# Two feed-forward layers with conditional mixing: NF4 levels by eight parametric ReLUs, condition matrices picked on VectorE

## The reference, cut to what matters

```
x = x + ffn0(cond0(x));   x = x + ffn1(cond1(x))
cond:  W = weights[condition]          # 16 matrices of 64x64; condition: one code 0..15 for each of 32 batches
       y[b] = W[b]^T x[b]              # einsum('bct,bcd->bdt')
ffn0:  y @ (ternary(w) * column scale) + b       # w 1024x1024
ffn1:  w = NF4_LEVELS[q_weight] * group scale    # q_weight 1024x1024 int32, codes 0..15; 64 values to a group
       y @ w^T + bias + 4 * lora
```

## Time and profile before

| | |
|---|---|
| time, 3 runs | median 371.6 us (371.12 to 373.02) |
| the profiled execution | 371.03 us, of which the span of the trace is 369.2 us |
| PE busy | 354.6 us (96%) |
| DVE, ACT, POOL busy | 243.3, 169.6, 228.3 us |
| mean granted TensorE clock | 0.994 |

### The profile page before, as it was taken

The page is one execution under the profiler, slowest core; times in us unless marked ns, Lnnn a source line. Parts: engine busy times, 40 slices in busy tenths (PEclk is TensorE's granted clock), DMA queues, the critical chain, the costliest instruction groups (busy, mean ns, idle before and its releaser), DMA issues.

```text
span 369.2 us, 5527 instructions
## 1 busy us (share of the span) xinstructions
PE 354.6 (96%) x1832; PEld 299.9 (81%) x1832; DVE 243.3 (66%) x361; ACT 169.6 (46%) x302; POOL 228.3 (62%) x147
## 2 busy tenths in 40 slices
PE   7999987999999999998989999999999999999996
PEld 6788875878888888887868888888888888888885
DVE  4996457587997887974699999846155362544522
ACT  4775647678888778882021323504013040231300
POOL 0769999956886878667443302386468464685642
PEclk9999999899999999999999999999999999999999
DMA  7994400554246146333331133021405014150202
GB/s 212 309 306 142 148 22 29 193 211 146 96 167 199 45 156 216 117 114 114 127 119 57 61 120 114 18 101 62 174 36 180 22 70 166 57 175 4 114 30 85
DMA packets 27838, 44.63 MB, mean 121 GB/s; under 512 B 8834, under 2 KB 17026, under 8 KB 27810
## 3 DMA queue, kind: packets, MB, share of 16 engines
q1 hardware_dynamic: 26466, 43.95, 34.9%
q10 hardware_dynamic: 1344, 0.33, 0.4%
HBM read 27.49 MB, written 16.78 MB: 120 GB/s over the span
## 4 chain that ended last, share of the span: by engine, by line
PE 73%; DVE 10%; ACT 6%; issue 4%; POOL 4%; DMA 1%; SPq 1%; DVEq 0%; POOLq 0%; ACTq 0%
PE acc L1177 31%; PE acc L1139 20%; PE xT L1103 9%; PE acc L1119 7%; PE spare L1103 3%; DVE plain_sums L927 3%; ACT spare L721 2%; POOL x_first L557 2%; DVE side_p L908 2%; DVE hl L865 2%; ACT hh L673 1%; PE acc L1204 1%; DMA mix<-in_L_cond_weights 1%; PE acc L1103 1%; POOL side_p L584 1%
## 5 line engine op out<-in xcount | busy, mean ns | idle before, releaser
L551 POOL TENSOR_TENSOR X<-X,bias 128x1024 f32<-128x1024 f32 x28 | 69.1, 2468 | 34.1 <-PE xT L1103 26.6
L1139 PE MATMUL acc<-T,hh 128*128 128x512 f32 x192 | 75.9, 396 | 0.0
L1139 PE MATMUL acc<-T,hl 128*128 128x512 f32 x192 | 75.0, 391 | 0.0
L721 ACT ACTIVATE spare<-q_mid 128x512 f32<-128x512 int8 x96 | 55.5, 596 | 13.6 <-DVE side_p L908 6.6
L1177 PE MATMUL acc<-W,hh 128*128 128x512 f32 x192 | 61.1, 389 | 0.0
L1103 PEld LDWEIGHTS xT<-mix,X 128*128 128x128 f32 x352 | 43.7, 197 | 7.4 <-issue 6.4
L1103 PE MATMUL xT<-mix,X 128*128 128x128 f32 x352 | 44.6, 282 | 4.2 <-DVE hl L865 4.1
L1010 DVE TENSOR_TENSOR X<-X,acc 128x512 f32<-128x512 f32 x36 | 24.7, 687 | 32.9 <-PE acc L1177 18.6
L1177 PEld LDWEIGHTS acc<-W,hh 128*128 128x128 f32 x192 | 36.0, 188 | 7.5
L1139 PEld LDWEIGHTS acc<-T,hl 128*128 128x128 f32 x192 | 36.1, 188 | 7.4
L1139 PEld LDWEIGHTS acc<-T,hh 128*128 128x128 f32 x192 | 36.1, 188 | 7.0
(11 more groups left out here) (97 smaller groups left out, 662.5 us busy)
## 6 DMA issues: line engine op xcount, KB each, us to landing
out<-X SPq DMA_DIRECT2D x26, 512.0 KB, 3.1
X<-out SPq DMA_DIRECT2D x16, 512.0 KB, 3.4
X<-in_x SPq DMA_DIRECT2D x12, 512.0 KB, 3.4
q_raw<-in_L_ffn_q_weight SPq DMA_DIRECT2D x16, 256.0 KB, 2.9
w_in<-in_L_ffn_w SPq DMA_DIRECT2D x15, 256.0 KB, 5.2
x_first<-in_x SPq DMA_DIRECT2D x4, 512.0 KB, 5.2
out<-x_first SPq DMA_DIRECT2D x4, 512.0 KB, 5.8
out<-X SPq DMA_DIRECT2D x4, 256.0 KB, 2.0
```

The costliest lines, as they stand in the source:

```text
L551: pool.tensor_tensor(x_of(g), x_of(g), bias[:, :], ALU.add).then_inc(s_xb, 1)
L721: act.activation(dst, q_mid[:, parity, :], ACT.Copy, scale=slope, bias=offset).then_inc(s_line, 1)
L1139: mm = pe.matmul(acc[:, bank_of(q), :], a[:, k, :], b, start=(k == 0 and j == 0), stop=(k == KB - 1 and j == len(terms) - 1))
```

## The change

Two things are changed together.

Codes to levels: a piece is now 128 x 1024, eight pieces in all, and ACT runs a chain of eight parametric ReLUs over it, each with its own scale, offset and slope below zero; the last one gives the levels. DVE has no part in it any more and POOL only multiplies by the scales. `turn_w` writes both halves into `spare`, and `high_w` and `low_w` take 1024 columns at once. acc uses its four banks in turn for all tiles of layer 0.

Condition matrices: the whole table of a layer (16 x 64 x 64) is loaded into both halves of the partitions. `tok` is loaded into all partitions, DVE compares it with 0 to 15 (`choose`), and `pick` copies, for each of the 16 conditions, the table's matrix into `picked` where the mask says so: 32 predicated copies for a group of tiles (one of 64 columns for a tile in the first two groups of two tiles, of 128 columns in the groups of four). ACT then copies the group to the diagonal blocks of `mix`, which now has 8 places (`place`, two operations).

```
+    GROUPS = [(0, 2), (2, 4)] + [(g, g + 4) for g in range(4, 2 * NT, 4)]
+    NPICK = 2 * NCOND
...
+            def place(i):
+
+                a, b = GROUPS[i]
+                act.wait_ge(s_picked, NPICK * (i + 1))
+                if i == 0:
+                    act.wait_ge(s_fill, 1)
+                need(act, s_xT, NH * (b - NM))
+                for h in range(2):
+                    rows = slice(h * C, (h + 1) * C)
+                    act.activation(mix[rows, a % NM:a % NM + b - a, rows], picked[rows, 0:b - a, :],
+                                   ACT.Copy).then_inc(s_mix, 1)
...
+                    act.activation(lev, src, ACT.Prelu, scale=scale, bias=offset, alpha=below
+                                   ).then_inc(s_lev, 1)
...
             act.preload_act_table(ACT.Sign)
-            act.wait_ge(s_tok, 16)
-            act.wait_ge(s_fill, 1)
-            load_condition(act, 0, 1)
-            load_condition(act, 1, 1)
+            load_table(act, mix0, 1)
             load_weights(act, 2, 0)
             act.dma_start(b_raw[:, :, :], lora_b_v).then_inc(s_bin, 16)
+            place(0)
+            place(1)
             signs(0, 0)
...
-            act.wait_ge(s_ain, 64)
-            act.activation(loraA[:, :], a_raw, ACT.Copy).then_inc(s_ah, 1)
-            per = (2 * NL + 1) * ND
+            per = NS * ND
+            place(group_of(F))
             for g in range(SB):
                 if g == 1:
                     colscale(1)
+                    act.wait_ge(s_ain, 64)
+                    act.activation(loraA[:, :], a_raw, ACT.Copy).then_inc(s_ah, 1)
...
+            def pick(i, start=0, stop=NPICK):
...
+                for u in range(start, stop):
+                    c, part = divmod(u, 2)
+                    t = a % NT + n * part
+                    mine = chosen[:, c, t:t + n].unsqueeze(2).to_broadcast([P, n, C])
+                    if c > 0:
+                        dve.wait_ge(s_picked, NPICK * i + u - 1)
+                    dve.copy_predicated(picked[:, n * part:n * part + n, :], mine,
+                                        table[:, c, :].unsqueeze(1).to_broadcast([P, n, C])
+                                        ).then_inc(s_picked, 1)
...
+            choose()
+            pick(0)
+            pick(1)
             ternary(0, 0)
...
             leave_y(2)
-            per = 2 * NC * ND
+            pick(group_of(F))
...
-                    if g < NT:
-                        maxima(share(per, m), share(per, m + 1))
-                    else:
+                    for i, (a, b) in enumerate(GROUPS):
+                        if a >= 2 * F and a - 4 <= g <= a - 3:
+                            at = NPICK // 4 * (m - NH * (a - 4))
+                            pick(i, at, at + NPICK // 4)
...
                 if p + 1 < NP:
                     low_A(p + 1, A22, 1)
+                if (SB + 2 * p + 4, SB + 2 * p + 8) in GROUPS:
+                    pick(group_of(SB + 2 * p + 4))
```

More of the change, by code:

```diff
@@ L42, with nf4_stages_are_right @@
 NF4_ZERO = 7
-def line_through(a, level_a, b, level_b):
-    f = np.float32
[L49 to L82, removed]
+NF4_STAGES = [(0.300930947, -1.00947642, 1.30589235), (0.999999046, -3.25468516, 0.532812595),
+              (1.00000417, 0.568540156, 0.82866317), (1.00000179, 0.706044614, 1.09465003),
+              (0.999996901, -1.0337441, 0.641103864), (0.999999702, 0.375342011, 0.934238434),
+              (0.999999046, 0.679873884, 2.33418441), (1.0, -0.545852602, 1.14412689)]
+def nf4_stages_are_right():
+    f = np.float32
+    for q in range(len(NF4_LEVELS)):
+        y = f(q)
+        for scale, offset, below in NF4_STAGES:
+            y = f(float(y) * float(f(scale)) + float(f(offset)))
+            y = y if y > 0 else f(y * f(below))
+        assert abs(float(y) - float(f(NF4_LEVELS[q]))) <= float(np.spacing(abs(f(NF4_LEVELS[q])))), q
+        assert y == 0 or q != NF4_ZERO
 def build(nc, x, itok, mix0, w0, b0, mix1, q_weight, q_scale, b1, lora_a, lora_b, out):
@@ L121, in build @@
     NP = (2 * NT - SB) // 2
-    assert C * 2 == P and NH == 2 and ND == NT and G == 16 and R == 8
-    above, below = nf4_lines()
+    assert C * 2 == P and NH == 2 and G == 16 and R == 8
+    nf4_stages_are_right()
     x_v = x.rearrange("(t s) c f -> t (s c) f", s=2)
@@ L174, in ready_in, with begun_in @@
     def ready_in(d):
-        return next(m for m in range(NH * NT) if share(2 * NC * ND, m + 1) >= 2 * NC * (d + 1))
+        return next(m for m in range(NH * NT) if share(NS * ND, m + 1) >= NS * (d + 1))
+    def begun_in(d):
+        return next(m for m in range(NH * NT) if share(NS * ND, m + 1) > NS * d)
     def turned_in(d):
@@ L210, in build @@
         mix = sb("mix", [P, NM, P], F32)
+        table = sb("table", [P, NCOND, C], F32)
+        with ExitStack() as first_use:
+            number = sb("number", [P, NCOND], I32, first_use)
+        picked = sb("picked", [P, 4, C], F32)
+        with ExitStack() as first_use:
+            ones = sb("ones", [P, P], F32, first_use)
         loraA = sb("loraA", [P, T], F32R)
@@ L321, in build @@
         s_bin = sem("s_bin")
-        s_qin = [sem(f"s_qin{k}") for k in range(2)]
+        s_qin = sem("s_qin")
         s_zero = sem("s_zero")
@@ L511, in _ @@
                     load_x(g + 3)
+                if g == 10:
+                    sp.wait_ge(s_picked, NPICK * G0)
+                    load_table(sp, mix1, 0)
+                    load_table(sp, mix1, 1)
+                for d in range(2, ND):
+                    if begun_in(d - 1) // NH == g:
+                        load_q(d)
             sp.wait_ge(s_xb, NT)
@@ L840, in _ @@
                                        ).then_inc(s_loraB, 1)
+                if g >= F and (g + 2, g + 6) in GROUPS:
+                    place(group_of(g + 2))
                 for m in (NH * g, NH * g + 1):
@@ L849, in _ @@
                     if g < NT:
-                        lines(share(per, m), share(per, m + 1))
+                        stages(share(per, m), share(per, m + 1))
                     else:
```

214 lines of the change are left out of this document (86 added, 128 removed).

## The result

| | before | after |
|---|---|---|
| median of 4 runs | 371.36 us (370.8 to 373.02) | 409.57 us (407.74 to 412.17) |
| profiled execution, its span | 371.03, 369.2 us | 407.74, 405.9 us |
| PE busy | 354.6 us (96%) | 365.8 us (90%) |

The ratio is 1.103 (95% interval 1.095 to 1.110): 38.2 us slower where 19.9 were forecast, and outside the range of 374 to 402.

The account below looks back on a forecast made before the run. PE, busy 354.6 of 369.2 us, was taken to set the end. Start, tiles 4 to 7, low clock and first rounds gave 19.2, later stalls -3.7, boundaries +4.4: 19.9 on 371.0, so 391.0 us, range 374 to 402.

Parts of the forecast that it names:

- Start, +8.65: Kernel start: table landing at 6.0 and 64 copies at 0.14 us delay the first sign; PE's first(0,0,1) 8.65 us later.
- Tiles 4 to 7, +8.95: At turn_b: copies held beside POOL delay ACT's place and colscale(1), so PE waits 8.95 us more.
- Low clock behind it, +1.7: After the wait at turn_b: PE wakes at the low clock level, costing 1.7 us.
- mixed(5), -1.66; scaled weights, -1.6; mixed(6), +3.2: First loop rounds: mixed(5)'s wait goes, the scaled-weights stall shrinks by 1.6 us, mixed(6) waits 3.2 us for its low part.
- Loop copies 0 (0 to 4): Loop: DVE, having lost 96 maxima, absorbs the copies at about zero cost, 0 to 4 us.
- Later stalls, -3.7: Later in the kernel: the stalls of 0.7, 1.3 and 1.78 us go, 3.7 us gained.
- Pair boundaries, +4.4: Boundaries between pairs: copies for tiles 24 and 28 delay freeing a bank, 2.2 us each, 4.4 us.
- 1 (DVE keeps the port): Tiles 4 to 7: overlapping copies never release the port, so POOL waits 6.6 us; 382.3 us, chance 0.2.
- 2 (no clash): Copies beside POOL: the mask is read another way, so nothing is held; 374.9 us, chance 0.17.
- 3 (faster): Whole kernel: relief exceeds the start's price, with 64-column copies in 0.075 us; 364.8 us, chance 0.1.
- Rival 4: All groups: as forecast, but each copy takes the full 0.25 us; about 405 us, chance 0.08.

Follow-up runs that it names:

- e3: Changed kernel with 4 copies in place of 32 in each of the first two groups; 403.18 us.
- f4: Changed kernel with the products' banks moved on by one and 4 copies in place of 32 in every group; 367.04 us.
- e8: Changed kernel with POOL waiting for the 32 copies of tiles 4 to 7 ahead of its first add_bias; 407.83 us.
- e4: Changed kernel with 4 copies in place of 32 in the group of tiles 4 to 7; 400.59 us.
- h3: Changed kernel with the products' banks moved on by one and 32 small matmuls on PE ahead of the wait for the column scale; 400.46 us.
- i2: Changed kernel with the products' banks moved on by one and 4 copies in place of 32 in the groups of tiles 8 to 19; 395.03 us.
- f6: Changed kernel with the products' banks moved on by one and 4 copies in place of 32 for tiles 20 to 23; 398.54 us.
- i3: Changed kernel with the products' banks moved on by one and 4 copies in place of 32 in the groups of tiles 8 to 23; 392.26 us.
- f1: Changed kernel with condition matrices loaded by DMA as before, Relu for parametric ReLU, and the products' banks moved on by one; 363.45 us, ratio 0.979 to before.
- i1: Changed kernel with the banks of the seven products moved on by one, timed; 402.4 us, ratio 1.084 to before.
- f3: Changed kernel with the banks of the seven products moved on by one, a single run; 402.88 us.
- h2: Changed kernel with the products' banks moved on by one and one wide copy per condition in place of two; 410.44 us.

## Why the prediction was wrong

Two steps failed. The copies in the loop were put at zero and cost 4 to 6 us where DVE was already full, and the relief of 3.7 us didn't show behind them. The bank of the last result was no term of the sum at all; it cost 4.3 us at its place. Going by its own steps:

- *Start, +8.65.* Right in kind, +10.8 at tile 3. The copies cost what was taken (0.136 from start to start for 0.14). The landing of the table was taken at 6.0 from the first weights and came at 7.7, and the second group's wait for `place(0)` (0.8) was overlooked. e3 and f4 split it: some 7.4 us are the copies, 3.4 the table and the rest.
- *Tiles 4 to 7, +8.95.* Right, and the step that was least certain. +10.2 from tile 3 to tile 4 is the wait of 8.07 and the low clock behind it. e8 shows the mechanism, e4 the amount.
- *Low clock behind it, +1.7.* There, but worth nothing at tile 6 (h3): the chain that sets mixed(6) runs over ACT, POOL and DVE and not over PE. The forecast's +19.2 at tile 6 doesn't hang on it, though. Without the 1.7 PE reaches the first scaled piece at 76.8 and not at 78.5, waits 2.7 for it and not 1.0, and all that follows stands where it stood. That is what h3 shows, 2.3 us of waiting for 0.4. So the spell changed the terms of the sum and not the sum. The wait of 8 us was right to count, because that same chain stood behind the same copies.
- *mixed(5), -1.66; scaled weights, -1.6; mixed(6), +3.2.* Right: 84.0 forecast for mixed(6), 84.78 measured; +19.9 for +19.2. A part of that closeness is luck: the copies of tiles 4 to 7 began 2.0 us later than forecast (43.26 for 41.3) and took 0.8 less (14.37 for 15.2).
- *Loop copies 0 (0 to 4).* Wrong. For tiles 12 to 19 it holds (under 1 us at tile 17 in i2). For tiles 20 to 23 it doesn't: 4 to 6 us (f6, i3). The copies are dealt out by tile, the last ones fall into tiles 16 and 17, and there DVE begins the block sums at 93% busy. "DVE has lost its 96 maxima and absorbs that" is true for tiles 8 to 13 and false behind it, since no maxima stood there. The earlier trace rows had shown the stage; its busy share was not read.
- *Later stalls, -3.7.* The relief is real: f1 is 8.1 us below before, where the three terms of relief made 7.0. In the changed kernel it doesn't show after tile 17, because DVE's lag replaced the stall of 1.78 at tile 18.
- *Pair boundaries, +4.4.* Right in place and mechanism; the two waits are 2.13 each for 2.2. The copies took 298.95 - 292.93 = 6.02 us after POOL's end, for 6.0. With the low clock behind each they cost 6.5 us in the changed kernel (tiles 22 to 28) and in i1, 4.9 in f3 and 4.8 in h3.
- *Missing: the bank of the last result.* 4.3 us at tile 22, and 7 us of the time as measured (1.103 to 1.084). The change to `bank_of` was in the diff, and only its first-layer half was taken up.

From tile 6 to the end the sum is: 0.7 ahead of it, 9.6 between tiles 6 and 21 (+5.9 instead of -3.7), 4.3 at the bank, 2.1 more at the boundaries: 16.7, the whole distance between +36.6 and +19.9. The median of four runs stands 1.8 us above the profiled one; that makes the rest.

Of the rivals, 1 (DVE keeps the port), 2 (no clash) and 3 (faster) are out by the rows above: POOL's operations stay at 2.45 and 1.40, the copies take 14.37 us. Rival 3's 0.075 us a copy was 0.136. Rival 4 (405) came nearest, for the wrong reason: the copies do overlap. The rule cited in the prediction, of the Trainium skill ("VectorE: DVE Perf Modes", The DRAIN you can't avoid), would have made the start's copies 0.22 apart; they are 0.136 apart. But the prediction quoted half of it: the same section says that a next operation which isn't held starts earlier, and that is what these rows show. By the other ("SBUF — State Buffer", Who interferes with whom) an instruction with two SBUF inputs shares an exclusive lock with GpSimd, and the trace agrees for a predicated copy too, which the page doesn't name: 14.37 us beside POOL, 7.82 with POOL mostly silent.

How the 7.4 us of i2 and the 4.3 of f6 divide between waits and the clock behind each wait is not settled. Single runs of kernels with the same start differ by up to 2.4 us at tile 3 (+10.8 in h3, +13.2 in f3), and the granted clock between 12 and 30 us is 1.00 in the one and 0.62 in the other; differences of 2 us between single runs carry no weight by themselves.

## What to carry to other kernels

Read the busy share of every engine by stage before saying that added work is absorbed: here copies cost under 1 us where they were dealt out to tiles 8 to 13, and some 6 in tiles 16 and 17. When a diff touches the assignment of buffers or banks, write down for each first use in the next stage who freed it last, and what that engine has queued ahead of it; a barrier of that kind also swallows every gain made before it, so a good change can measure as none (371.46 for 363.45). And count a low-clock spell only where the chain that sets the next wait runs through TensorE.

## What the runs showed of the hardware

- A predicated copy of 64 columns lasts 223 ns and starts 136 ns after the one before, where it doesn't wait for that one's end (changed kernel, start). 128 columns: 289 ns, 202 apart (32 copies, tiles 4 to 7, after POOL's end). 256 columns, where the program makes each wait for the last: 448 ns, some 480 apart (h2).
- Beside POOL's additions about one long copy passes at each end of a POOL operation, whatever its width (3 held at a boundary with 128 columns and with 256), up to 2.5 us each. POOL is hardly slowed (2.45 for 2.4).
- A Relu and a parametric Relu on ACT over 1024 f32 columns last the same, 1059 ns.
